# A fused Perceiver layer: who builds the identity, the inverse deviation and the cleared tiles before the first attention pair

## The reference

```python
x = x + xattn(layernorm(x), ctx, ctx)   # 16 heads of 64, 256 queries, 4096 keys, no mask
x = x + attn(layernorm(x))              # causal, 16 memory keys, heads mixed before and after the softmax
x = x + ffn(layernorm(x))               # gated, 4-bit weights and 16-bit activations emulated

def layernorm(x): return (x - mean(x)) / sqrt(var(x) + 1e-5)
def xattn(q, k, v):
    q, k, v = q @ w_q, k @ w_k, v @ w_v          # split into heads
    return merge_heads(softmax(q @ k.T / 8) @ v) @ w_o
```

## Time and profile before

| | before |
|---|---|
| median of 3 runs | 1374.15 us |
| the profiled execution's own time | 1373.69 us |
| its span | 1371.9 us |
| mean granted TensorE clock | 0.968 |
| TensorE busy | 1266.9 us (92%) |
| ScalarE busy | 880.6 us (64%) |
| VectorE busy | 865.2 us (63%) |
| Pool busy | 411.3 us (30%) |

### The profile page before, as it was taken

One profiled execution on the slowest core, in us unless ns is written; L12 is line 12 of the kernel. 1 busy time (PEld: TensorE's weight loads), 2 busy tenths in 40 slices (PEclk: granted clock), 3 DMA queues, 4 the chain that ended last, 5 costly groups with the idle time before them and its releaser, 6 DMA issues. The chain is left out here.

```text
span 1371.9 us, 21416 instructions
## 1 busy us (share of the span) xinstructions
PE 1266.9 (92%) x8447; PEld 1004.7 (73%) x8447; DVE 865.2 (63%) x1121; ACT 880.6 (64%) x1543; POOL 411.3 (30%) x373
## 2 busy tenths in 40 slices
PE   4999999999999999999999999999999969898663
PEld 3887887878787878697878787878887734667422
DVE  4547575766766576736766766576757645657366
ACT  5858586867777776766867777776868412535242
POOL 4506061524334342321524334242515022030000
PEclk9999999999999999999999999999999979998876
DMA  5000000000000011200000000000000063352000
GB/s 172 1 2 20 1 20 1 20 1 20 11 10 16 1 36 47 81 1 1 20 0 20 14 8 20 1 20 2 16 1 4 1 202 58 38 68 33 1 0 16
DMA packets 29683, 34.62 MB, mean 25 GB/s; under 512 B 3984, under 2 KB 26000, under 8 KB 29328
## 3 DMA queue, kind: packets, MB, share of 16 engines
q1 hardware_dynamic: 27536, 29.83, 8.4%
q0 software_dynamic: 2048, 3.43, 1.8%
HBM read 25.89 MB, written 0.52 MB: 19 GB/s over the span
## 5 line engine op out<-in xcount | busy, mean ns | idle before, releaser
L505 DVE TENSOR_TENSOR prob_sum<-prob_sum,probs 128x1024 f32<-128x1024 f32 x224 | 261.7, 1222 | 171.0 <-ACT probs L426 170.3
L341 POOL TENSOR_TENSOR k_split<-probs,k_split 64x512 fp32r<-64x512 f32 x128 | 164.5, 1285 | 359.0 <-ACT probs L388 357.5
L482 DVE TENSOR_REDUCE step_max<-scores_a 128x2 f32<-128x1024 f32 x128 | 156.7, 1224 | 96.7 <-PE scores_a L608 96.7
L343 POOL TENSOR_TENSOR k_split<-probs,k_split 64x512 fp32r<-64x512 f32 x128 | 164.6, 1286 | 9.6
L426 ACT ACTIVATE probs<-scores_a 128x1024 f32<-128x1024 f32 x98 | 100.5, 1026 | 93.8 <-PE scores_a L621 93.8
L482 DVE TENSOR_REDUCE step_max<-scores_b 128x2 f32<-128x1024 f32 x128 | 155.7, 1217 | 0.0
L426 ACT ACTIVATE probs<-scores_b 128x1024 f32<-128x1024 f32 x98 | 100.6, 1027 | 55.9 <-PE scores_b L621 55.9
L333 POOL TENSOR_TENSOR w_lo<-w_raw,w_hi 128x768 fp32r<-128x768 f32 x16 | 38.4, 2400 | 298.3 <-ACT w_hi L355 298.2
L632 PE MATMUL out_ps<-probs,v_far 128*64 128x256 f32 x1024 | 118.0, 382 | 0.0
L632 PE MATMUL out_ps<-probs,v_near 128*64 128x256 f32 x1024 | 118.0, 382 | 0.0
L620 PE MATMUL scores_a<-q_twice,k_split 128*128 128x256 f32 x392 | 100.3, 288 | 0.2 <-ACT probs L426 0.2
(11 more groups left out here) (218 smaller groups left out, 2866.0 us busy)
## 6 DMA issues: line engine op xcount, KB each, us to landing
ctx_rows<-in_ctx_dram SPq DMA_DIRECT2D x10, 512.0 KB, 3.9
w_raw<-in_L_xattn_w_v_dram SPq DMA_DIRECT2D x14, 256.0 KB, 3.4
probs<-in_ctx_dram SPq DMA_DIRECT2D x6, 512.0 KB, 6.2
grouped<-dots_sb SPq DMA_DIRECT2D x16, 136.0 KB
grouped<-dots_sb POOLq DMA_DIRECT2D x16, 136.0 KB, 13.2
w_raw<-in_L_xattn_w_q_dram SPq DMA_DIRECT2D x16, 128.0 KB, 2.4
w_raw<-in_L_xattn_w_k_dram SPq DMA_DIRECT2D x16, 128.0 KB, 2.6
wo_pair<-in_L_xattn_w_o_dram SPq DMA_DIRECT2D x16, 128.0 KB, 2.1
```

What stands on the lines that cost most here:

```text
L341: pool.tensor_tensor(k_split[DH:P, A, keys], staged[0:DH], k_split[0:DH, A, keys].bitcast(F32), ALU.subtract).then_inc(k_low, 1)
L343: pool.tensor_tensor(k_split[0:DH, B, keys], staged[DH:P], k_split[DH:P, B, keys].bitcast(F32), ALU.subtract).then_inc(k_low, 1)
L482: dve.tensor_reduce(step_max[:, :, 1 - h, j - 1], scores[h][:, :, :], X, ALU.max).then_inc(max_done, 1)
L505: dve.tensor_tensor(prob_sum[:, h, :], prob_sum[:, h, :], probs[:, j % 2, h, :], ALU.add).then_inc(sum_done, 1)
```

## The change

The identity moves to VectorE. It clears `ident`, builds a ramp 0 to 31 along the free axis of a 32-column tile by five doublings, transposes it in blocks of 32, and compares ramp and transposed ramp for each of the four 32x32 blocks on the diagonal. The inverse deviation is now an add on VectorE, a square root on ScalarE and a reciprocal on VectorE. The clear of side B of `k_ones` is a ScalarE copy with scale 0; Pool keeps the clear of side A, which now waits for the identity only, and then writes both rows of ones; the last ScalarE fill is gone. ScalarE splits the first weights after the fourth context group in place of the sixth. At the end of its list in this block Pool runs one `affine_select` on a tile that nothing reads afterwards.

```diff
 NORMALISED = 3 * TOK_TILES
 
 
-def normalise_rows(dve, x, out, stats, moments, chain, inverse_std):
-
-
+def measure_rows(dve, x, stats, moments, chain):
     n = 0
     for t in range(TOK_TILES):
         dve.bn_stats(stats[:, t, :], x[:, t, :]).then_inc(chain, 1)
     dve.wait_ge(chain, n)
     for t in range(TOK_TILES):
         dve.bn_aggr(moments[:, t, :], stats[:, t, :]).then_inc(chain, 1)
-    n += TOK_TILES
+
+
+def scale_rows(dve, x, out, moments, chain, inverse_std):
+    n = 2 * TOK_TILES
     dve.wait_ge(inverse_std, 3)
     for t in range(TOK_TILES):
         dve.tensor_scalar(out[:, t, :], x[:, t, :], moments[:, t, 0:1], moments[:, t, 1:2],
                           ALU.subtract, ALU.mult).then_inc(chain, 1)
     assert n + TOK_TILES == NORMALISED
+
+
+def normalise_rows(dve, x, out, stats, moments, chain, inverse_std):
+    measure_rows(dve, x, stats, moments, chain)
+    scale_rows(dve, x, out, moments, chain, inverse_std)
 
 
 def invert_std(pool, moments, power, chain, inverse_std):
     PAIR = 2 * DH
     V_TILES = HALF // STEPS
     A, B = 0, 1
+    BLOCK32 = 32
+    RAMP = [1, 2, 4, 8, 16]
+    IDENT = 2 + len(RAMP) + 1 + P // BLOCK32
 
     with ExitStack() as stack:
         r = Resources(nc, stack)
...
-        power = r.sbuf("power", [P, TOK_TILES])
...
+        ramp = r.sbuf("ramp", [P, 2, BLOCK32])
...
-        ones_a = r.sem("ones_a")
+        cleared_b = r.sem("cleared_b")
...
 
         @block.gpsimd
         def _(pool):
-            pool.memset(ident[:, :], 0.0).then_inc(ident_made, 1)
-            pool.wait_ge(ident_made, 1)
-            pool.affine_select(out=ident[:, :], in_=ident[:, :], compare_op=ALU.not_equal, fill=1.0, base=0,
-                               pattern=[[-1, P]], channel_multiplier=1).then_inc(ident_made, 1)
             pool.memset(ones[:, :], 1.0).then_inc(consts_ready, 1)
             pool.memset(neg_max[:, :, :], 0.0).then_inc(consts_ready, 1)
-            invert_std(pool, moments, power, norm_chain, inverse_std)
-            pool.wait_ge(norm_chain, NORMALISED)
+            pool.wait_ge(consts_ready, 2)
+            pool.wait_ge(ident_made, IDENT)
             pool.memset(k_ones[DH:P, A, :].bitcast(F32), 0.0).then_inc(consts_ready, 1)
             pool.wait_ge(consts_ready, 3)
-            pool.memset(k_ones[0:DH, B, :].bitcast(F32), 0.0).then_inc(consts_ready, 1)
+            pool.wait_ge(norm_chain, NORMALISED)
+            pool.memset(k_ones[DH:DH + 1, A, :].bitcast(F32), 1.0).then_inc(consts_ready, 1)
             pool.wait_ge(consts_ready, 4)
+            pool.wait_ge(cleared_b, 1)
             pool.memset(k_ones[0:1, B, :].bitcast(F32), 1.0).then_inc(consts_ready, 1)
 
             def body(it, b, i, parity):
...
             for b in range(BATCH):
                 pairs_of_batch(pool, b, body)
 
+            pool.affine_select(out=ramp[:, 0, :], in_=ramp[:, 0, :], compare_op=ALU.is_ge, fill=0.0, base=0,
+                               pattern=[[1, BLOCK32]], channel_multiplier=-1).then_inc(consts_ready, 1)
+            pool.wait_ge(consts_ready, 6)
+
         @block.scalar
         def _(act):
             def split_weights(it, b, i):
...
                     context_high(act, next_group(b, i, STEPS))
             for b in range(BATCH):
                 if b == 0:
+                    act.wait_ge(consts_ready, 1)
+                    act.activation(k_ones[0:DH, B, :], ones[0:DH, 0:1].to_broadcast([DH, CTX]), ACT.Copy, scale=0.0
+                                   ).then_inc(cleared_b, 1)
+                    act.wait_ge(inverse_std, 1)
+                    act.activation(moments[:, :, 1], moments[:, :, 1], ACT.Sqrt).then_inc(inverse_std, 1)
                     for n in range(LOADS):
                         context_high(act, n)
-                        if n == LOADS - 3:
+                        if n == 3:
                             split_weights(0, 0, 0)
-                    act.wait_ge(consts_ready, 5)
-                    act.activation(k_ones[DH:DH + 1, A, :], ones[DH:DH + 1, 0:1].to_broadcast([1, CTX]), ACT.Copy
-                                   ).then_inc(ones_a, 1)
                 pairs_of_batch(act, b, body)
 
         @block.vector
         def _(dve):
+            dve.memset(ident[:, :], 0.0).then_inc(ident_made, 1)
+            dve.memset(ramp[:, 0, 0:1], 0.0).then_inc(ident_made, 1)
+            for n, w in enumerate(RAMP):
+                dve.wait_ge(ident_made, 2 + n)
+                dve.tensor_scalar(ramp[:, 0, w:2 * w], ramp[:, 0, 0:w], float(w), None, ALU.add
+                                  ).then_inc(ident_made, 1)
+            dve.wait_ge(ident_made, 2 + len(RAMP))
+            dve.transpose(ramp[:, 1, :], ramp[:, 0, :]).then_inc(ident_made, 1)
+            dve.wait_ge(ident_made, 2 + len(RAMP) + 1)
+            for n in range(P // BLOCK32):
+                block32 = slice(n * BLOCK32, (n + 1) * BLOCK32)
+                dve.tensor_tensor(ident[block32, block32], ramp[block32, 0, :], ramp[block32, 1, :], ALU.is_equal
+                                  ).then_inc(ident_made, 1)
             dve.wait_ge(x_loaded, 16)
-            normalise_rows(dve, x_res, xn, stats, moments, norm_chain, inverse_std)
+            measure_rows(dve, x_res, stats, moments, norm_chain)
+            dve.wait_ge(norm_chain, 2 * TOK_TILES)
+            dve.tensor_scalar(moments[:, :, 1], moments[:, :, 1], EPS, None, ALU.add).then_inc(inverse_std, 1)
+            dve.wait_ge(inverse_std, 2)
+            dve.reciprocal(moments[:, :, 1], moments[:, :, 1]).then_inc(inverse_std, 1)
+            scale_rows(dve, x_res, xn, moments, norm_chain, inverse_std)
 
             def divide(before):
 
...
         @block.tensor
         def _(pe):
             mm = pe.matmul
-            pe.wait_ge(ident_made, 2)
+            pe.wait_ge(ident_made, IDENT)
 
             def transpose_context(n):
 
...
 
                 if is_first(it):
                     pe.wait_ge(consts_ready, 5)
-                    pe.wait_ge(ones_a, 1)
                 pe.wait_ge(max_chain, 2 * it + 2)
                 for qt in range(QT):
                     last = pe.transpose(k_ps[0][:, qt * P:(qt + 1) * P], neg_max[:, qt, :], ident[:, :])
...
```

## The result

The changed kernel took 1366.81 us (median of 5 runs, 1364.34 to 1367.92) against 1374.99 us for the kernel before (5 runs, 1373.31 to 1376.01): a ratio of 0.9946, 95% interval 0.9930 to 0.9962. Its profiled execution took 1366.61 us with a span of 1364.8. The forecast was 1368.7, faster.

A forecast was written before the change was run, and what follows sets the result against it. Pool's code fetch and clears, then ScalarE's fill, were taken to hold the first key copy at 32.88 us. Moving it 6.3 earlier, less 0.8 for clock, gave 5.5: 1368.2 profiled, 1368.7 median; range 1364.5 to 1372.7.

The forecast's parts named there:

- The deciding step: On Pool behind the clears: a code fetch of 7.0 us remains before `w_lo`, which then starts at 23.0.
- the upper bound that I drew: Pool's code fetch was priced between 5.94 and 11.09 us, or nothing if it belongs to `affine_select` alone.
- the fifth of the distance above 5.94: Pool's fetch before `w_lo`: a fifth added towards 11.09, for the last context load and other code, giving 7.0 us.
- The small terms: Before the first key product: identity 3.2, normalised x 8.9, clears to 16.0, `w_lo` to 24.85, key product 24.9 us.
- the slack that I set against the second table load: At the first exponential: the 1.28 us load makes it 0.67 late, against 0.70 slack; nothing taken, upper end 0.7.
- The drain that the Trainium skill adds: ScalarE table loads at about 2.7 us each with drain: exponential 2.1 us late, sum 1.4 higher; not taken.
- the clock: TensorE, idle before `w_lo`, runs the first two key products slowly: 0.8 us lost, bounds 0 and 1.5.
- the context groups: VectorE's context chain runs from 8.9 to 21.8 us, all ready by 22, ahead of `w_lo`.
- the sum: First key copy 6.3 us earlier, less 0.8 for TensorE's clock: 5.5 us against the profiled execution.
- the forecast's own range: 1366.7 to 1371 us, from a fetch of 5.9 to 8.5, clock 0 to 1.5 and `w_lo` up to 2.40.
- E: In the ten microseconds after the first key copy, slow TensorE replaces ScalarE as bound: 1.5 us left, 1372.6; chance 0.06.

The follow-up runs named there:

- the run with the late rows: The changed kernel with Pool writing the two rows of ones after pair 0's low parts, leaving one clear before `w_lo`; 1362.66 us, ratio 0.9906.
- The late split: The changed kernel with ScalarE splitting the first weights after the sixth context group again, not the fourth; 1368.43 us, ratio 0.9950.

## Why the prediction was right

**The deciding step** (the fetch stands before Pool's first instruction that isn't a memset) held: 7.10 us against 7.0 taken. Where Pool reaches that instruction at about 16 us, it lasts 6.71 to 7.10 in four profiles; where it does so in the first 2 us, 10.58 to 11.09 in eight; and the run with the late rows has 11.58 from 6.84 us on, a little over the upper bound that I drew. That the gap is a fetch of code remains a reading: the runs show where it stands and how long it is. What I could not tell, whether it waits for `w_hi`, is settled: it doesn't. Without Pool's wait for x the clears ended at 14.00, and `w_lo` started at 23.48, 0.16 after `w_hi` was done, so the fetch had passed in the meantime. The size was in part luck: the fifth of the distance above 5.94 was put there for the last context load, and from 16.05 to 23.14 us the DMA share was 0.01.

**The small terms** held within 0.1 us: identity at 3.21 (3.2), the root started as soon as its table was in (7.02 after a load to 7.00), normalised x at 8.85 (8.9), clears to 16.04 (16.0), `w_lo` 1.79, first key product at 24.99 (24.9). The exponential came 0.70 later than the shift of the steps around it (67.09 for 72.99, but 71.34 for 76.54), and `w_hi` after it only 0.15: the slack that I set against the second table load was there. The drain that the Trainium skill adds (ScalarE: Activation LUTs, What ACT_TABLE_LOAD costs) isn't seen: 1.28 at 70.05, and the exponential starts at 71.34.

**Mis-sized: the clock.** I took 0.8 us for the first key product; it was 1.04 (2.54 for 1.50), and filling TensorE's wait gave it back. I also did not see that a first slow stretch would fall on the last transposes, from 18.5 us: VectorE was done with the context groups at 23.69, not 21.8. It cost nothing here, since `w_lo` was later still.

**Two errors that cancel.** The first key copy moved by 5.11 us, 0.4 less than the sum says, and at the second pair the lead was 5.75: 0.64 was gained between the two, for which the sum has no term. It arises behind the first `v_far` copies (42.15 for 47.26, still 5.11; the second ones 46.12 for 51.78, 5.66); why wasn't tried. That 5.75 is so near to 5.5 is thus in part luck. The upper end of the forecast's own range comes to about 1371.4 by its terms, not 1371.

**The medians** moved by 8.2, not 5.5, and 1366.81 lies at the lower edge of the forecast's own range (1366.7 to 1371). The interval of the ratio covers 5.2 to 9.6 us, so the runs don't show that the excess is real. Two candidates were looked at. One may cover most of it: the profile on which the sum was built has the earlier prologue of the two. Against the second one the lead at the second pair is 7.6 us, not 5.75, and the profiled times, 1373.69 and 1375.39, lie on either side of the median; two profiles don't tell which is the common case. The other doesn't: the changed kernel's profile had no slow stretch at the change of batch (1.8 us); but the same kernel without the last `affine_select` had one, and its profiled time, 1366.75, and its median, 1366.87, are those of the changed kernel. So the cause of the excess stays open. E, the rival of a head start given back, is not what happened.

**Which part brought it.** In medians ScalarE's fill moved, alone on the kernel before, brings 5.8. On the changed kernel the root undone costs 1.5 and the identity undone 1.4, each from ten runs and against medians of 1366.81 (five) and 1366.87 (eight, without the last `affine_select`); the ratios' intervals still overlap, so the sizes are rough. The late split stands 1.6 above the changed kernel, from three runs, with nothing in its profile to carry it: not told from noise. The last `affine_select` brings nothing. The parts are not to be added: the identity alone on the kernel before brought nothing, as fill, `w_lo` and context groups bound one after another. ScalarE's clear of side B, which takes one 3.5 us clear off Pool, was never undone by itself.

## What to carry to other kernels

A gap before a GpSimd instruction that nothing explains is not that instruction's own: moved away, it shows up before the next one that isn't a memset, so take it early or where something else is late anyway, and take long memsets out of the path beside it: the two rows of ones, moved behind pair 0, were worth 4.2 us more. Look first for the engine that fills its list with something nobody needs yet: one fill of 3.6 us, moved, gave 5.8 of the 8.2 us of the whole rewrite. And an early start that ends in a wait was paid for in TensorE clock, 1.1 us here. Last, one profile of each kernel is not enough for a difference of 2 us: two profiles of the same kernel differed by 1.8 in the prologue alone.

## What the runs showed of the hardware

- Pool's 4096-column memset and VectorE's tensor_scalar from SBUF to SBUF did not run side by side: 3680 ns for one of 128x256 where 394 to 401 is normal, and 7.31 us for four beside two memsets. The memset itself stays at 3.50 to 3.54. VectorE's subtractions with a PSUM operand ran beside the same memsets at their usual 1.28 for two, and bn_stats (1.41 for four) too.
- TensorE's first transposes take 1.94 us for eight where 1.06 is normal, while the granted clock reads 1.00. The phase had ended by 16.9 us in one profile of the kernel before and lasted to about 20 in the other; what ends it was not tried.
- Pool's gap before its first instruction that isn't a memset is about 4 us longer when it lies under the opening loads (10.58 to 11.58 us, against 6.71 to 7.10 from 16 us on). A tensor_tensor has it at both lengths (10.70 and 7.10), so the kind of instruction isn't the reason; that the loads are was not tried, as no run changed them.
